# Graph block with batch norm and gated relational layers: loads of x and W on SP's queue and split by partition, turns and x times W earlier, weight merges and parts in other places

## The chip, the cores and the metric

The kernel runs on one core of a Trainium2 chip. The metric is the device time of one execution in microseconds (us). Time of the kernel before: 353.66 us, the median of three runs (353.53 to 355.02). TensorE (PE) multiplies, VectorE (DVE), ScalarE (ACT) and GpSimd (POOL) compute elementwise, SyncE (SP) only issues loads and stores; ScalarE and GpSimd issue some too.

## The reference

625 nodes with 512 features, 20,625 directed edges (`src`, `dst` sorted by `dst`, a type of 0 or 1 each). Cut to what matters:

```python
# layer 0, edges src -> dst
xw  = x @ W.T
deg = segment_sum(1, dst');  dinv = rsqrt(deg)         # dst' also holds one more loop per node
h   = segment_sum(dinv[row] * dinv[col] * xw[row], col) + b
h   = gelu(batch_norm(h, gamma, beta), exact);  x1 = layernorm(x + (h + x))
# layer 1, twice (first with relu behind it)
w[r] = sum_b att[r, b] * basis[b]                      # 2 relations, 30 bases of 512 x 512
msg  = (sigmoid(x_j @ gate_w[r]) * x_j) @ w[r]         # r = type of the edge, x_j = features of dst
out  = segment_sum(msg, src) + x @ root + bias
return layernorm(x1 + out)
```

## The kernel before

Matrix products in 32 bits are made of three: each operand is split into a part `hi` of reduced precision and the rest `lo` (`mm3`, lines 469 to 471).

**The edge stage.** The 20,625 edges are 162 tiles of 128, in 27 groups of 6. For each tile VectorE makes a one-hot matrix of keys (`oh_key`, 128 x 320, line 1037), where a key joins the chunk of the source node (5 chunks of 125 nodes), the type and the place of the destination in a window of 32 nodes that begins at the group's smallest destination (its base). The one-hot of the source's place inside its chunk (`oh_src`) comes from ScalarE for four tiles of a group (`places`, line 773) and from VectorE for two (line 1035). TensorE multiplies the two (line 560) into one of two banks, and VectorE adds the window into the count matrix `B` (`add_window`, line 1022). `oh_key` has 12 slots, `oh_src` three groups. Before the first tile VectorE needs: the edges, turned by TensorE (line 506), the places inside the chunk (line 956 on; ScalarE waits for these), the minimum and maximum of each group (line 967), S, the coefficients for the basis sums (line 975), a few scalars that say whether further rounds are needed (lines 981 to 987), the base on all partitions (lines 524 and 989) and the keys (lines 992 to 998).

**The basis sums** run through the whole kernel. The 64 parts of 1 MB each are loaded by SP's queue into a ring of four (line 371), each load when the part four before it has been used. A part is eight products (`basis_part`, line 476) that TensorE does at written-out places (`basis_upto(n)`). Four parts make a half, eight make one weight block: ScalarE takes the first half out of the bank (`w_first`), VectorE merges the second (`w_merge`, lines 1001 to 1010), ScalarE makes the `hi` part (`w_high`) and VectorE the `lo` part (`w_low`). The first part of a half waits for the half two before it to have left its bank.

**x and W** (the name `W0` in the code, `w_raw` in the profile) are loaded on ScalarE's queue behind the edges (lines 739 and 740), each in one transfer of 125 or 128 partitions. TensorE turns the 5 chunks of x and 4 blocks of W (`turn`) in nine places of the edge loop (`TURN_AT`: after groups 2, 4, 6, ..., 19), ScalarE evicts each one group later (`turned_parts`: a `hi` and a full copy) and GpSimd makes the `lo` part (line 418). x times W is twenty parts, two in each of the groups 14 to 23 (`FIRST_XW`). The first x turn stands after group 2, ahead of its basis part.

**Degrees and z.** From B the adjacency `AT` is made (line 1083), its column sums by TensorE (line 590); VectorE copies them, GpSimd raises five columns to the power -0.5 at once (line 423), VectorE makes the diagonals, ScalarE and VectorE scale x times W (`z`, hi line 827, lo line 1097), TensorE spreads the diagonals (line 600), and the aggregation follows (line 612). Then batch norm, gelu, residual sum, layer norm (five chunks, lines 1154 to 1167), turns of the result x1 (`x1_turned`), its `hi` and `lo` parts, and the products with root (line 652 on), which wait for the `lo` part of the first three chunks.

**The order** is written out by hand on each engine: an engine takes its instructions in order and waits on counters. The psM banks (four) go round in the order of the `use(...)` calls, so a turn also waits until the bank four uses before it has been evicted. The five result chunks are stored from SP's queue, one transfer of 250 KB each, when each is normalised (line 382).

Lines that the steps touch:

```python
340    FIRST_XW = 14
341    TURN_AT = dict(zip((2, 4, 6, 8, 10, 12, 15, 17, 19), range(len(turned))))
408    nc.gpsimd.memset(B[:].bitcast(F32), 0.0).then_inc(consts, 1)
423    nc.gpsimd.tensor_tensor(dinv_p[:], deg[:], mhalf[0:PC, 0:NC], ALU.pow)
567    basis_upto(LEAD + 4 * g // 5)          # LEAD = 3; in the loop over groups g
643    for c in range(EARLY):                 # EARLY = 3
644        x1_turned(c)
645        basis_upto((35, 36, 37)[c])
```

## Time and profile before

| | |
|---|---|
| median of 3 runs | 353.66 us (353.53 to 355.02) |
| the profiled execution | 356.38 us, its span 354.5 us |
| busy, of the span | TensorE 295.9, VectorE 184.2, ScalarE 138.2, GpSimd 51.8 us |
| mean granted clock of TensorE | 0.929 of 2.4 GHz |
| moved by DMA | 73.66 MB, 208 GB/s over the span |

The profile is of one execution; times are from the start of its span. The chain of waits goes back from the last instruction to what released each step; the table by stages gives each engine's busy time in a stretch, the clock that TensorE was granted, the mean share of the core's 16 DMA engines that were busy and the rate. The timeline lists instructions, with like ones merged (x16); in brackets stands how long the engine was idle before and what released it. PE is TensorE's multiplications, PEld its weight loads, ACTq and SPq are the queues of ScalarE and SP.

### The profile page before, as it was taken

The numbers are of one execution on the slowest core, as the hardware profiler recorded it, in microseconds if no ns is written. First come the engines' busy times: TensorE is split into PE (matmuls) and PEld (weight loads), VectorE is DVE, ScalarE is ACT, GpSimd is POOL, SyncE is SP. The second block draws the span as 40 slices with busy tenths as digits, with TensorE's granted clock in tenths as the row PEclk, the third lists the DMA queues.
The fourth block names the chain that finished last, engine by engine and source line by source line (L and its number), as shares of the span: only waits on it lengthen the run. The fifth ranks groups of instructions, "written<-read, shape, count | busy, mean of one in ns | idle before, by whom it ended". The sixth has DMA issues, their size and how long they took to land.

```text
span 354.5 us, 4839 instructions
## 1 busy us (share of the span) xinstructions
PE 295.9 (83%) x1709; PEld 195.7 (55%) x1709; DVE 184.2 (52%) x511; ACT 138.2 (39%) x273; POOL 51.8 (15%) x81
## 2 busy tenths in 40 slices
PE   0662398679999779964899999999999899999980
PEld 0321144346665648742466665556779577777760
DVE  6756079998997864568741013233245325333342
ACT  0064179896997032874823411411131332200000
POOL 5010021311110082027200000000000710010000
PEclk9986579899999759997899999999999999999996
DMA  6799278787577868971999957999200320000111
GB/s 242 292 283 328 96 275 319 251 305 264 203 285 269 325 206 307 336 274 66 329 388 421 379 160 275 358 358 327 92 2 0 87 64 0 2 0 25 32 31 59
DMA packets 12613, 73.66 MB, mean 208 GB/s; under 512 B 1808, under 2 KB 2051, under 8 KB 4396
## 3 DMA queue, kind: packets, MB, share of 16 engines
q1 hardware_dynamic: 9980, 68.49, 53.0%
q0 software_dynamic: 1104, 2.36, 2.5%
q10 hardware_dynamic: 1504, 2.49, 2.2%
q8 instruction: 14, 0.23, 0.3%
q14 instruction: 11, 0.09, 0.1%
HBM read 72.05 MB, written 1.28 MB: 207 GB/s over the span
## 4 chain that ended last, share of the span: by engine, by line
PE 67%; DMA 11%; ACT 7%; DVE 6%; issue 5%; POOL 2%; ACTq 1%; DVEq 0%; POOLq 0%
PE psW L488 15%; DMA xs<-in_x_dram 11%; PE psM L469 10%; PE psM L471 9%; PE psM L470 9%; PE psM L706 6%; PE psM L726 5%; PE psE L560 5%; PE psM L612 3%; ACT oh_diff L776 3%; POOL root_lo L438 1%; DVE AT L1083 1%; PE psM L669 1%; PE psM L639 1%; ACT w L771 1%
## 5 line engine op out<-in xcount | busy, mean ns | idle before, releaser
L488 PE MATMUL psW<-basis_ring,S 128*32 128x512 f32 x512 | 74.1, 671 | 1.6 <-DVEq L980 1.4
L1037 DVE TENSOR_SCALAR oh_key<-iota_f,key 128x320 f16<-128x320 f16 x162 | 45.9, 321 | 20.7 <-PE psE L560 16.9
L1197 DVE SCALAR_TENSOR_TENSOR zg<-psM,gate,zg 125x512 fp32r<-125x512 f32 x20 | 15.0, 750 | 60.3 <-ACT zg L894 60.3
L560 PEld LDWEIGHTS psE<-oh_key,oh_src 128*125 128x125 f16 x162 | 21.7, 148 | 33.9 <-ACT oh_src L782 20.2
L560 PE MATMUL psE<-oh_key,oh_src 128*125 128x320 f16 x162 | 31.5, 333 | 10.5 <-ACT oh_src L782 10.3
L776 ACT ACTIVATE oh_diff<-iota_f,edgeT 128x128 f16<-128x128 f16 x108 | 34.3, 389 | 1.7 <-ACT xT_full L790 0.9
L469 PE MATMUL psM<-w,hlT 128*125 128x512 f32 x80 | 32.7, 409 | 0.1
L894 ACT ACTIVATE zg<-psM,gate 125x512 fp32r<-125x512 f32 x20 | 13.8, 688 | 47.1 <-PE psM L471 46.7
L471 PE MATMUL psM<-w,hlT 128*125 128x512 f32 x80 | 31.6, 395 | 0.0
L470 PE MATMUL psM<-w,hlT 128*125 128x512 f32 x80 | 31.6, 395 | 0.0
L706 PEld LDWEIGHTS psM<-BB,zg 125*128 125x128 f32 x160 | 23.1, 188 | 4.2 <-DVEq L1220 3.4
L488 PEld LDWEIGHTS psW<-basis_ring,S 128*32 128x32 f32 x512 | 12.1, 116 | 23.9 <-issue 21.6
L706 PE MATMUL psM<-BB,zg 125*128 125x320 f32 (+1 forms) x160 | 24.4, 309 | 0.0
L726 PE MATMUL psM<-zg,BB 125*125 125x512 f32 x100 | 24.0, 394 | 0.0
L453 POOL DMA_DIRECT2D root_raw<-in_L_gnn_root_dram x16 | 7.9, 501 | 104.3 <-DVE hlT L1223 104.1
L726 PEld LDWEIGHTS psM<-zg,BB 125*125 125x125 f32 x100 | 18.6, 186 | 4.7
L469 PEld LDWEIGHTS psM<-w,hlT 128*125 128x125 f32 x80 | 14.8, 185 | 11.3 <-issue 5.0
L782 ACT ACTIVATE oh_src<-oh_diff,ones_f 128x512 f16<-128x512 f16 x27 | 19.5, 722 | 0.9
L1020 DVE TENSOR_TENSOR w<-w_both,w 128x512 fp32r<-128x512 f32 x16 | 14.2, 930 | 10.7 <-ACT w L771 10.4
L471 PEld LDWEIGHTS psM<-w,hlT 128*125 128x125 f32 x80 | 14.8, 186 | 3.8
L470 PEld LDWEIGHTS psM<-w,hlT 128*125 128x125 f32 x80 | 14.8, 186 | 3.2
L1035 DVE TENSOR_SCALAR oh_src<-iota_f,edgeT 128x128 f16<-128x128 f16 x54 | 15.3, 283 | 0.5 <-DVE w_both L1008 0.5
(161 smaller groups left out, 445.4 us busy)
## 6 DMA issues: line engine op xcount, KB each, us to landing
basis_ring<-in_L_gnn_basis_dram SPq DMA_DIRECT2D x64, 1024.0 KB, 6.4
root_raw<-in_L_gnn_root_dram POOLq DMA_DIRECT2D x32, 64.0 KB, 2.3
xs<-in_x_dram ACTq DMA_DIRECT2D x1, 1250.0 KB
out_dram<-xs SPq DMA_DIRECT2D x5, 250.0 KB
w_raw<-in_L_gnn_W_dram ACTq DMA_DIRECT2D x1, 1024.0 KB, 39.5
bias_b<-in_L_gnn_bias_dram POOLq DMA_DIRECT2D x1, 250.0 KB, 3.6
rows_i<-in_dst_dram SPq DMA_DIRECT2D x1, 80.0 KB
rows_i<-in_src_dram ACTq DMA_DIRECT2D x1, 80.0 KB
```

The costliest lines, as they stand in the source:

```text
L469: nc.tensor.matmul(o, l_hi, r_hi, start=start, stop=False)
L470: nc.tensor.matmul(o, l_hi, r_lo, start=False, stop=False)
L471: last[0] = nc.tensor.matmul(o, l_lo, r_hi, start=False, stop=stop)
L488: m = nc.tensor.matmul(psW[32 * j:32 * j + 32, cc % 2, :], S[:, cc % 2, cc // CH, q].rearrange("p k r -> p (k r)"), ring[:, n % RING, j, : ...
L560: nc.tensor.matmul(psE[0:PC, g % 2, 0:KEYS], oh_src[:, g % 3, j * P:j * P + PC], oh_key[:, t % OH, :], start=(j == 0), stop=(j == G - 1)). ...
L706: last[0] = nc.tensor.matmul(bank(("h", f, h))[:, 0:n], zg[:, i, d, r, f * P:(f + 1) * P], BB[:, at:at + n], start=(d + r + i == 0), stop= ...
L726: last[0] = nc.tensor.matmul(bank(("out", c))[0:PC, :], BB[:, at:at + PC], zg[:, i, d, r, :], start=False, stop=(d == NC - 1 and r + i == 2))
L776: nc.scalar.activation(oh_diff[:, g % 3, j * P:(j + 1) * P], iota_f[:, 0:P], ACT.Abs, bias=edgeT[:, 0, g * G + j:g * G + j + 1], scale=-1. ...
L782: nc.scalar.activation(oh_src[:, g % 3, 0:GA * P], oh_diff[:, g % 3, :], ACT.Relu, bias=ones_f[:, 0:1], scale=-1.0).then_inc(src_ready, 1)
L1035: v.tensor_scalar(oh_src[:, t // G % 3, t % G * P:(t % G + 1) * P], iota_f[:, 0:P], edgeT[:, 0, t:t + 1], None, ALU.is_equal)
L1037: v.tensor_scalar(oh_key[:, t % OH, :], iota_f[:, 0:KEYS], key[:, t:t + 1], None, ALU.is_equal) \
L1197: link(v.scalar_tensor_tensor(out=zg[:, 1, c, r, :], in0=bank(("Z", L, c, r))[0:PC, :], scalar=gate[:, L, c, r:r + 1], in1=zg[:, 0, c, r, ...
```

## The change

1. The loads of x and W move from ScalarE's queue to SP's, behind the destination edges and ahead of the basis. x is loaded in two transfers (`WIDE` = 112 and 13 partitions), and each of the five stores of the result becomes two in the same way.
2. Turns 0 and 1 (now chunks 0 and 1 of x) stand first on TensorE, ahead of the base product; then the product for the attention coefficients, two turns of W, and the other five turns after groups 0 to 4. ScalarE evicts turns 0 and 1 before the places of group 0, and the others after the places of groups 0 to 6.
3. x times W is in groups 4 to 13. The basis parts run up to `9 * g // 10` after group g, where it was `3 + 4 * g // 5`. Both end at part 23. The first two weight blocks' steps move to later groups, `w_first(2)` behind the loop.
4. ScalarE clears B, before its places; GpSimd did. VectorE waits for it before the first window addition.
5. On VectorE the minima and maxima come ahead of the chunks, and S and the rounds' scalars behind tile 11's keys. S is made by 8 instructions in place of 16 and a clearing.
6. The power for dinv is five instructions, one per column, and the diagonals and z go chunk by chunk behind them. `w_merge(2)` moves from before the copy of the degrees to behind the copies of `dinv_b`.
7. `w_merge(3)` moves from behind chunk 1 of the layer norm to behind chunk 4. On GpSimd the `lo` parts of root: two ahead of the layer norm's chunks, and one each behind chunks 1 and 2 (three ahead and one behind chunk 1 before).
8. Basis parts up to 35 stand ahead of x1's turns; 36 and 37 then fall to the place of 38 and 39.
9. GpSimd's permuted copy of the vectors moves behind its `lo` parts.

```diff
-        turned = [("xT", 0)] + [("w0T", k) for k in range(KC)] + [("xT", c) for c in range(1, NC)]
+        turned = [("xT", 0), ("xT", 1)] + [("w0T", k) for k in range(KC)] + [("xT", c) for c in range(2, NC)]
...
-        FIRST_XW = 14
-        TURN_AT = dict(zip((2, 4, 6, 8, 10, 12, 15, 17, 19), range(len(turned))))
...
-        FIRST_AT = {2: 0, 13: 1, 23: 2}
-        HIGH_AT = {9: 0, 20: 1}
-        MERGE_AT = {8: 0, 18: 1}
-        LOW_AT = {10: 0, 21: 1}
+        FIRST_XW = 4
+        FIRST_TURNS = 4
+        FIRST_AT = {8: 0, 17: 1}
+        HIGH_AT = {13: 0, 22: 1}
+        MERGE_AT = {11: 0, 20: 1}
+        LOW_AT = {14: 0, 23: 1}
...
             edge_rows(sp, 1, dst)
+            for p in (slice(0, WIDE), slice(WIDE, PC)):
+                sp.dma_start(xs[p], x.rearrange("(c p) o -> p c o", p=PC)[p]).then_inc(x_in, 16)
+            sp.dma_start(w0_raw[:], W0.rearrange("(c p) o -> p c o", p=P)).then_inc(w0_in, 16)
...
-                sp.dma_start(out.rearrange("(c p) o -> p c o", p=PC)[:, c], xs[:, c]).then_inc(out_done, 16)
+                for p in (slice(0, WIDE), slice(WIDE, PC)):
+                    sp.dma_start(out.rearrange("(c p) o -> p c o", p=PC)[p, c], xs[p, c]).then_inc(out_done, 16)
...
-            nc.gpsimd.memset(B[:].bitcast(F32), 0.0).then_inc(consts, 1)
...
-            nc.gpsimd.tensor_tensor(dinv_p[:], deg[:], mhalf[0:PC, 0:NC], ALU.pow).then_inc(dinv_ready, 1)
+            for c in range(NC):
+                nc.gpsimd.tensor_tensor(dinv_p[:, c:c + 1], deg[:, c:c + 1], mhalf[0:PC, 0:1], ALU.pow).then_inc(dinv_ready, 1)
...
-            for k in range(KC - 1):
-                root1_low(k)
+            root1_low(0)
+            root1_low(1)
             for c in range(NC):
...
-                if c == 1:
-                    root1_low(KC - 1)
+                if 1 <= c < KC - 1:
+                    root1_low(c + 1)
...
-            basis_upto(LEAD)
+            for i in range(2):
+                turn(i)
+            pe.wait_ge(base_ready, 1)
...
+            for i in range(2, FIRST_TURNS):
+                turn(i)
             for g in range(NG):
...
-                if g in TURN_AT:
-                    turn(TURN_AT[g])
+                if g + FIRST_TURNS < len(turned):
+                    turn(g + FIRST_TURNS)
...
-                basis_upto(LEAD + 4 * g // 5)
+                basis_upto(9 * g // 10)
...
-            pe.wait_ge(diag_ready, 1)
             for h, (c0, c1) in enumerate(((0, 4), (4, NC))):
                 wait_free(pe, ("dinv", h))
                 for c in range(c0, c1):
+                    pe.wait_ge(diag_ready, c + 1)
...
+            basis_upto(35)
             for c in range(EARLY):
                 x1_turned(c)
-                basis_upto((35, 36, 37)[c])
...
-            act.dma_start(xs[:], x.rearrange("(c p) o -> p c o", p=PC)).then_inc(x_in, 16)
-            act.dma_start(w0_raw[:], W0.rearrange("(c p) o -> p c o", p=P)).then_inc(w0_in, 16)
...
+            counts = B[:].rearrange("p s t n -> p (s t n)").bitcast(F32)
+            nc.scalar.activation(counts, ones_f[0:PC, 0:1].broadcast_to(list(counts.shape)), ACT.Copy, scale=0.0) \
+                .then_inc(b_zero, 1)
...
+            turned_parts(0)
+            turned_parts(1)
+            act.wait_ge(place_ready, 1)
             for g in range(NG):
                 places(g)
...
-                if g in EVICT_AT:
-                    turned_parts(EVICT_AT[g])
+                if g + 2 < len(turned):
+                    turned_parts(g + 2)
+            w_first(2)
...
+                if t == 2 * G - 1:
+                    build_S()
+                    rounds()
+                    dve.wait_ge(b_zero, 1)
...
-            w_merge(2)
             wait_full(dve, "deg")
...
             for c in range(NC):
-                last = v.tensor_scalar(diag[:, c, :], ident[0:PC, 0:PC], dinv_p[:, c:c + 1], None, ALU.mult)
-            last.then_inc(diag_ready, 1)
-            for c in range(NC):
+                dve.wait_ge(dinv_ready, c + 1)
+                v.tensor_scalar(diag[:, c, :], ident[0:PC, 0:PC], dinv_p[:, c:c + 1], None, ALU.mult).then_inc(diag_ready, 1)
                 dve.wait_ge(z_hi, c + 1)
...
+            w_merge(2)
...
-                if c == 1:
-                    w_merge(3)
+            w_merge(3)
```

## Rows read from the trace of the kernel before

**Rows 1.** The chain that ended last: start in us, length in us, what.

```profile
3.75 37.80 DMA xs<-in_x_dram
...
114.38 0.97 PE psE L560 x6
...
129.84 1.87 PE psW L488 x8
...
172.28 0.99 PE psW L488 x8
...
174.33 0.39 PE psM L469
```

**Rows 2.** Windows of 1 us: each engine's busy time, clock, DMA share, GB/s.

```profile
36.00:37.00 1.00, 0.00 (x0) 0.00 (x0) 0.00 (x0) 0.00 (x0) 0.00 (x0) 0.50 0.34 139
...
350.00:351.00 1.00, 0.00 (x0) 0.00 (x0) 0.00 (x0) 0.00 (x0) 0.00 (x0) 0.50 0.33 100
```

**Rows 3.** Table by stages: us, busy PE, PEld, DVE, ACT, POOL, clock, DMA, GB/s.

```profile
77.65:110.47 32.82, 32.78 (x197) 20.68 (x198) 29.25 (x103) 28.90 (x69) 3.99 (x3) 1.00 0.70 250
...
157.67:174.33 16.66, 11.05 (x65) 5.15 (x65) 13.95 (x33) 10.31 (x13) 9.60 (x14) 0.80 0.53 191
...
174.33:199.52 25.19, 25.19 (x177) 16.43 (x178) 7.18 (x12) 9.62 (x18) 0.00 (x0) 1.00 1.00 395
```

**Rows 4.** Timeline of the start: start, length, engine, line, what [idle before].

```profile
2.52 2.83 POOL L408 MEMSET B<- 125x3280 f32 x1
...
2.58 2.85 DVE L929 CAST ident<-ident 128x128 bf16<-128x128 f32 x1 [2.44 <-POOL BB L407]
...
4.36 16.35 ACTq L740 DMA_DIRECT2D w_raw<-in_L_gnn_W_dram  x1
...
7.25 0.56 DVE L940 CAST rows_f<-rows_i 81x768 f32<-81x768 int32 x1
...
13.11 1.65 DVE L975 TENSOR_TENSOR S<-mask_k,psM 128x32 f32<-128x32 f32 x16 [0.47 <-PE psM L518]
...
16.13 0.19 DVE L989 COPY base_b<-psM 128x27 f32<-128x27 f32 x1
...
17.98 0.94 DVE L1037 TENSOR_SCALAR oh_key<-iota_f,key 128x320 f16<-128x320 f16 x4
```

**Rows 5.** Timelines of ScalarE and VectorE in the edge stage.

```profile
52.78 1.26 ACT L776 ACTIVATE oh_diff<-iota_f,edgeT 128x128 f16<-128x128 f16 x4
...
55.97 1.28 ACT L776 ACTIVATE oh_diff<-iota_f,edgeT 128x128 f16<-128x128 f16 x4 [0.20 <-ACT w0T_full L790]
...
77.45 0.47 DVE L1027 TENSOR_TENSOR B<-B,psE 125x320 f32 x1
...
79.69 0.48 DVE L1027 TENSOR_TENSOR B<-B,psE 125x320 f32 x1
```

**Rows 6.** Timelines of GpSimd and VectorE in the edge stage.

```profile
75.57 1.27 POOL L418 TENSOR_TENSOR xT_lo<-xT_full,xT_hi 128x500 fp32r<-128x500 f32 x1 [4.99 <-ACTq L795]
...
75.66 1.24 DVE L1035 TENSOR_SCALAR oh_src<-iota_f,edgeT 128x128 f16<-128x128 f16 x1
...
78.51 0.25 DVE L1035 TENSOR_SCALAR oh_src<-iota_f,edgeT 128x128 f16<-128x128 f16 x1
```

**Rows 7.** Timelines of TensorE, VectorE and GpSimd, 120 to 156 us.

```profile
120.24 3.31 PE L590 MATMUL psM<-ones_r,AT 125*125 125x2 f32 x15 [0.19 <-DVE AT L1085]
...
122.19 0.74 DVE L1004 SCALAR_TENSOR_TENSOR w_both<-psW,mask_h,w_half 128x512 f32<-128x512 f32 x1
...
124.60 0.17 DVE L1088 COPY deg<-psM 125x5 f32<-125x5 f32 x1 [0.24 <-DVE w_both L1008]
...
124.99 1.20 POOL L423 TENSOR_TENSOR dinv_p<-deg,mhalf 125x5 f32<-125x5 f32 x1 [24.57 <-DVEq L1090]
...
134.13 0.49 DVE L1119 TENSOR_TENSOR hf<-psM,dinv_b 128x320 f32<-128x320 f32 x1 [2.50 <-PE psM L612]
...
155.48 0.54 POOL L420 TENSOR_TENSOR bn<-bn,mhalf 128x1 f32<-128x1 f32 x1 [2.79 <-DVE bn L1128]
```

More of the change, by code:

```diff
@@ L72 @@
 EPS = 1e-5
+WIDE = PC // 16 * 16
 SWAPPED = [i ^ 1 for i in range(32)]
@@ L242, in gnn_block @@
         use("minmax", "dve")
+        turned = [("xT", 0), ("xT", 1)] + [("w0T", k) for k in range(KC)] + [("xT", c) for c in range(2, NC)]
+        for name in turned[0:2]:
+            use(name, "act")
+        use("base", "dve")
         use("att", "dve")
-        use("base", "dve")
-        turned = [("xT", 0)] + [("w0T", k) for k in range(KC)] + [("xT", c) for c in range(1, NC)]
-        for name in turned[0:KC + 2]:
+        for name in turned[2:]:
             use(name, "act")
@@ L250, in gnn_block @@
             use(("xw", c), "act")
-            if KC + 2 + c < len(turned):
-                use(turned[KC + 2 + c], "act")
         use("vec", "act")
@@ L513, in _ @@
             done()
-            pe.wait_ge(att_in, 16 * 2)
-            pe.wait_ge(spread_ready, SUB)
-            wait_free(pe, "att")
-            for q in range(SUB):
-                last[0] = nc.tensor.matmul(bank("att")[:, 2 * R * q:2 * R * (q + 1)],
-                                           spread[:, q * P:(q + 1) * P],
-                                           att_t[:].rearrange("p l r -> p (l r)"), start=True, stop=True)
-            done()
-            pe.wait_ge(base_ready, 1)
-            wait_free(pe, "base")
-            last[0] = nc.tensor.matmul(bank("base")[:, 0:NG], ones_f[0:1, :], gmm[0:1, 0, :], start=True, stop=True)
-            done()
             def turn(i):
                 what, c = turned[i]
-                pe.wait_ge(x_in if what == "xT" else w0_in, 16)
+                pe.wait_ge(x_in if what == "xT" else w0_in, 32 if what == "xT" else 16)
                 wait_free(pe, (what, c))
@@ L543, in xw_part @@
                 n = slice(c * PC, (c + 1) * PC)
-                pe.wait_ge(in_lo, 2 + k if c == 0 else 1 + KC + c)
+                pe.wait_ge(in_lo, 3 + k if c == 0 else 1 + KC + c)
                 if k == 0:
@@ L550, in xw_part @@
                     done()
-            basis_upto(LEAD)
+            for i in range(2):
+                turn(i)
+            pe.wait_ge(base_ready, 1)
+            wait_free(pe, "base")
+            last[0] = nc.tensor.matmul(bank("base")[:, 0:NG], ones_f[0:1, :], gmm[0:1, 0, :], start=True, stop=True)
+            done()
+            pe.wait_ge(att_in, 16 * 2)
+            pe.wait_ge(spread_ready, SUB)
+            wait_free(pe, "att")
+            for q in range(SUB):
+                last[0] = nc.tensor.matmul(bank("att")[:, 2 * R * q:2 * R * (q + 1)],
+                                           spread[:, q * P:(q + 1) * P],
+                                           att_t[:].rearrange("p l r -> p (l r)"), start=True, stop=True)
+            done()
+            for i in range(2, FIRST_TURNS):
+                turn(i)
             for g in range(NG):
@@ L931, in _ @@
             v.tensor_reduce(mask_h[:], ident[:].rearrange("p (j k h) -> p h j k", j=JB, h=2), AX.XY, ALU.add)
[L932 to L934 removed]
+            v.tensor_reduce(mask_k[:], ident[:].rearrange("p (b k) -> p k b", k=KB), AX.X, ALU.add)
             v.tensor_reduce(pair_sum[:], ident[0:2 * R, 0:2 * R].rearrange("p (i r) -> p r i", r=R), AX.X, ALU.add)
@@ L953, in _ @@
                 dve.sem_inc(free_dve, 1)
+            wait_full(dve, "minmax")
+            for i, op in enumerate((ALU.min, ALU.max)):
+                last = v.tensor_reduce(gmm[0:1, i, :], bank("minmax")[0:1, i * ROWS:(i + 1) * ROWS]
+                                       .rearrange("p (g t) -> p g t", t=G // 2), AX.X, op)
+            link(last)
+            dve.sem_inc(free_dve, 1)
+            dve.sem_inc(base_ready, 1)
             chunk = beyond
```

67 lines of the change are left out of this document (27 added, 40 removed).

## The prediction

> **What bounds the kernel now.** I read the table by stages first, then the chain of waits, then the timeline of each engine where two stages meet. The chain opens with the load of x: issued at 3.75 us, it ends the wait of the tensor engine only at 41.6 [rows 1]. While it finishes alone, the DMA share is 0.34 at 139 GB/s, about 5 of 16 engines; where basis loads fill the queue from 174 us on, the share is 1.00 and the rate 395 GB/s [rows 3]. x's destination has 125 partitions and the outputs' too: near the end the same share, 0.33, at 100 GB/s comes back [rows 2]. W's load, issued behind x on ScalarE's queue, takes 16.35 us to issue and keeps ScalarE from its first instruction [rows 4]. After that come an edge stage of 27 groups of six one-hot products (to 115.4 us [rows 1]), the degree and z stage, the first aggregation, the residual and layer norm, and from 174.33 us a stretch in which the tensor engine is busy all the time [rows 3] to 344.6.
>
> In the edge stage three engines are close. VectorE needs 2.24 us for a group (one window addition to the next, 77.45 to 79.69), ScalarE 3.19 for a group's places with the eviction of one turned chunk (52.78 to 55.97) [rows 5]. The ten groups that also hold x times W took 32.82 us with the tensor engine busy throughout [rows 3]: with them it is the bound.
>
> **1. Loads of x and W** go to SP's queue ahead of the basis and x splits into 112 and 13 partitions. x is 1.28 MB. If the large part uses all engines at 395 GB/s, it takes 3.2 us; issued at about 2.0 to 2.6, and one or two microseconds until data flows and is confirmed (an estimate), it lands near 7.7 (bounds: 6, and 14 if the split does nothing, see the rivals). W needs 1.05 MB more, 2.6 us, and lands near 10.3; basis part 0 near 13. A part of the basis is first wanted at about 18, so the 5 us that it is later costs nothing. SP passes three more issues before its first basis load, ScalarE two fewer. For splitting speaks the low share of both transfers with 125 partitions [rows 2]. The Trainium skill, page "DMA: Bandwidth & Descriptors", section "Why a DMA increments its semaphore by 16 and not by 1", has a load use the largest number up to 16 that divides its outermost size: 5 for 125, 16 for 112, 13 for 13, and the trace agrees with the first. The same page's "Rules for kernel authors" speaks against the change: halves by partition serialize, so one is told not to split; that is a rival below.
>
> **2. Start of VectorE.** Its first cast takes 2.85 us although it is 128 elements wide; it ends with GpSimd's clearing of B, 2.83 us, 2.52 to 5.35 [rows 4]. The clearing moves to ScalarE, idle then; VectorE saves about 2.6. The edge lists are then the limit. They are issued ahead of everything else, and the trace doesn't show when they land, only that the conversion at 7.25 [rows 4] finds them there: it starts between 0 and 2.6 earlier; I take 2.0, near the upper end, as they are small loads, 80 KB each. Building S (1.65) and the rounds' scalars leave the path to the keys: from the start of S at 13.11 to the copy of the base at 16.13, 3.0 us, they are all that stood before the base [rows 4], and S had waited some 0.4 for the attention load. So 3.4 off. First key at 17.98 - 2.0 - 3.4 = 12.6. The base product now stands behind the turns of x chunks 0 and 1, done by about 10 if x lands at 7.7, so it waits for nothing. ScalarE: table load, B, two evictions of turned chunks (until about 12), places of group 0 (about 2): first product at about 14; before, ScalarE's queue was free only at 20.7 [rows 4].
>
> **3. Edge stage.** Groups 0 to 4, by VectorE: two groups without their additions, 2 x (2.24 - 0.47) = 3.5 [rows 5], plus two GpSimd low parts. Such a part slows VectorE: during the one at 75.57 a VectorE instruction that else takes 0.25 takes 1.24 [rows 6], so 1.0 each. 12.6 + 3.5 + 2.0 = 18.1. S and rounds, 3.0: 21.1. Three more groups at 2.24 + 1.0: 30.8. ScalarE needs 3.19 a group and would be at group 4 by 27, the tensor engine likewise: VectorE decides. Group 4's products end at 30.9. The ten groups with x times W (now 4 to 13) hold nine basis parts where they held eight, 32.8 + 1.0, less 1.0 for group 4's own products, already counted: group 14 opens at 63.7. By then VectorE is two groups ahead (twelve key slots). Groups 16 to 26: 11 x 2.24 = 24.6, a weight merge 2.4 [rows 7] and a low part, taken alike, 2.4: 93.1, and 0.5 for the last group. The basis has 12 parts to bring there at 2.6 each, 31 us, mostly ahead in the ring: no bound. **End 93.6 against 115.4: -21.8.** Bounds: 88 (VectorE not slowed by GpSimd, half the S block hidden) and 101 (basis and VectorE waits adding up, 0.5 a group).
>
> **4. z stage.** The merge leaves the path: VectorE copies the degrees at 124.60 after the merge that began at 122.19, but the degree products run until 123.5 [rows 7], so 1.0 comes off, not 2.4. The power of five columns takes 1.21 us [rows 7]; a single one 0.54 [rows 7], so the first result comes 0.7 earlier and the last 1.5 later. VectorE then does diagonal and low z of a chunk in 0.9, so chunk 4's diagonal is ready at 128.7, and after one product and the basis part of 1.87 [rows 1] the aggregation starts at 131.1, where that part ended at 131.7: **-0.6** (bounds -1.5, 0). The merge lands in VectorE's wait of 2.50 us before 134.13 [rows 7]: nothing. Without that wait it would cost 2.4 at the basis part that needs it.
>
> **5. Layer norm.** VectorE has 13.95 us of work in these 16.66 [rows 3], and the low part of turned chunk 2 is what the products at 174.33 [rows 1] wait for. The merge moves from chunk 1 to behind chunk 4, still ahead of that low part: the same work before the same instruction. GpSimd's two low parts later let chunk 0 through 1.3 earlier, but VectorE is still late: 0. Parts 36 and 37 ran here in the tensor engine's idle time and now stand in the stretch where it is always busy: 2 x 0.99 [rows 1] = **+1.9**. And the tensor engine now does its two parts at 160, then only three short turns before 174.3. The mean granted clock of 0.80 over 16.66 us [rows 3] is 6.7 us at 1.2 GHz, at which eight basis products take 1.87 and not 0.99 [rows 1]. Before, basis parts used those slow microseconds up; now root's products meet them, about 5 us at half speed: **+2.5** (bounds 0, 3.3).
>
> **6. End.** Five stores become ten. The last two chunks' 0.5 MB take some 5.1 us at 100 GB/s [rows 2]; over all engines at 395 GB/s 1.3, and one more issue of 0.26: **-3.5** (bounds -2.5, -3.9).
>
> **Sum.** -21.8 - 0.6 + 1.9 + 2.5 - 3.5 = -21.5. The profiled execution took 356.38 us (span 354.5), so 334.9; the median of the runs is 353.66, 2.7 lower, and the same step from there gives **332.2, called 332**.
>
> **Rivals.**
> A. *The edge stage gives back only the wait*: what was late because of x goes, and the earlier start is eaten by VectorE, GpSimd and basis waits. Edge end at 101 or a little later, 14 off the edge stage instead of 22, 339.6. For it: VectorE is busy 29.25 of 32.82 us [rows 3]. Against: twelve slots of slack.
> B. *The split does nothing for the rate*: x alone at 115 GB/s or so takes 11, ahead of the basis in its queue, landing at 13.5; the start shifts by 5.8 and the stores save nothing, 3.5: 332 + 9.3 = 341. By the skill's rule on halves this is the case. Against: share 0.33 [rows 2] leaves eleven engines free.
> C. *Slower than before*: the base product, and so every key, now waits for x, where three groups ran without it. If x still lands at 41.6, sharing engines with W and the basis, the whole edge stage moves by 33.6: 365. It decides once x lands after about 29.5. Against: x is first in its queue, not beside others.
> D. *More than I think*: VectorE runs groups 0 to 4 unslowed and the clock after layer norm costs nothing: 27 off for the edge and 0 for the clock: 324.
>
> **Chances.** Forecast (326 to 336) 0.55, A 0.22, B 0.06, C 0.03, D 0.14. About 0.5% is what a measurement can tell here. Only C is slower; within 0.5% would need A to lose 13 us more, 0.01. So faster 0.96, same 0.01, slower 0.03. Range: from D's edge to A and B, 324 to 342; outside is some 0.12.
>
> **What would show it.** x's turn before 10 us; first one-hot product near 14; ScalarE's queue without a 16 us issue; x times W in groups from 30 to 64; end of the edge stage at 93; VectorE without the 2.85 us cast; in the layer norm a tensor engine idle for some 5 us before root's first products, and those at 1.2 GHz; DMA share in the stores near 1 and the last one done within 2.5 us of the issue. The prediction is wrong if x lands after 12, or if the ten groups with x times W take more than 36, or the last thirteen more than 32.

## The result, and the profile after

The changed kernel took 339.75 us (median of four executions, 338.11 to 342.25), the kernel before 354.34 on the same chip (353.53 to 355.26): a ratio of 0.959, 95% interval 0.953 to 0.966. The forecast was 332 within 324 to 342. The sum was made for one profiled execution each: 356.38 before, 338.11 after, so 18.3 less where 21.5 were forecast. The medians lie only 14.6 apart: the profiled execution before was the slowest of its kernel, the one after the fastest. So the time lies in the stated range, but outside the forecast's own 326 to 336 and next to rival A's 339.6, whose mechanism did not happen (below).

Page of the changed kernel: span, busy time, DMA share in 40 slices.

```profile
span 336.3 us, 4839 instructions
...
PE 295.1 (88%) x1709; PEld 195.7 (58%) x1709; DVE 180.5 (54%) x502; ACT 141.1 (42%) x274; POOL 50.4 (15%) x84
...
DMA  6968799699997898660899678988000410000111
```

TensorE has the same work (295.9 us before), in a span 18 us shorter. Its chain of waits (start, us, what):

```profile
2.39 8.23 DMA xs<-in_x_dram
...
149.91 5.22 issue
...
160.11 5.77 DMA basis_ring<-in_L_gnn_basis_dram
```

The wait for x is 8.2 us long and ends at 10.6; it was 37.8 us long and ended at 41.6 [rows 1]. New are 5.22 us in which TensorE stands still ahead of root's products, and a basis part that it waits for at 166. The timeline of all engines, where stages meet:

```profile
5.10 2.94 ACT L803 ACTIVATE B<-ones_f 125x3280 f32<-125x3280 f32 x1
6.34 0.56 DVE L948 CAST rows_f<-rows_i 81x768 f32<-81x768 int32 x1 [2.35 <-DMA rows_i<-in_edge_type_dram]
...
10.66 1.93 PE L524 MATMUL psM<-ident,xs 125*128 125x125 f32 x8 [2.24 <-DMA xs<-in_x_dram]
13.25 0.19 DVE L981 COPY base_b<-psM 128x27 f32<-128x27 f32 x1 [1.34 <-PE psM L547]
13.58 0.98 DVE L984 TENSOR_TENSOR key<-edgeT,base_b 128x162 f32<-128x162 f32 x1
14.31 1.28 ACT L780 ACTIVATE oh_diff<-iota_f,edgeT 128x128 f16<-128x128 f16 x4 [0.19 <-ACT xT_full L794]
14.60 1.18 DVE L988 TENSOR_SCALAR key<-key 128x162 f32<-128x162 f32 x1
16.54 0.94 DVE L1050 TENSOR_SCALAR oh_key<-iota_f,key 128x320 f16<-128x320 f16 x4
...
22.36 1.94 PE L491 MATMUL psW<-basis_ring,S 128*32 128x512 f32 x8 [2.28 <-DVEq L1001]
...
96.31 0.49 DVE L1040 TENSOR_TENSOR B<-B,psE 125x320 f32 x1 [0.86 <-PE psE L566]
104.41 0.17 DVE L1104 COPY deg<-psM 125x5 f32<-125x5 f32 x1 [1.31 <-PE psM L596]
104.82 3.43 POOL L426 TENSOR_TENSOR dinv_p<-deg,mhalf 125x1 f32<-125x1 f32 x5 [65.47 <-DVEq L1106]
...
166.02 1.07 PE L491 MATMUL psW<-basis_ring,S 128*32 128x512 f32 x8 [0.99 <-DMA basis_ring<-in_L_gnn_basis_dram]
```

And its table by stretches (busy time and instructions of PE, PEld, DVE, ACT, POOL, then granted clock, DMA share, GB/s); the last row is the stores:

```profile
5.00:6.00 1.00, 0.00 (x0) 0.00 (x0) 0.00 (x0) 0.99 (x2) 0.00 (x0) 1.00 1.02 309
...
8.00:9.00 1.00, 0.42 (x4) 0.07 (x1) 0.68 (x3) 0.03 (x1) 0.00 (x0) 1.00 1.19 226
9.00:10.00 1.00, 0.00 (x0) 0.00 (x0) 0.63 (x3) 0.00 (x0) 0.00 (x0) 1.00 1.11 125
...
34.00:44.00 10.00, 10.00 (x61) 5.72 (x60) 9.55 (x30) 9.68 (x25) 3.43 (x3) 1.00 0.78 279
...
64.00:74.00 10.00, 10.00 (x72) 4.46 (x70) 9.23 (x40) 9.32 (x24) 0.00 (x0) 1.00 0.94 338
...
139.23:155.13 15.90, 6.17 (x44) 3.57 (x43) 13.92 (x34) 11.47 (x16) 9.61 (x14) 0.78 0.51 198
155.13:158.63 3.50, 3.50 (x14) 3.46 (x15) 1.99 (x2) 0.13 (x1) 0.00 (x0) 0.53 0.00 0
...
333.00:334.00 1.00, 0.00 (x0) 0.00 (x0) 0.16 (x1) 0.00 (x0) 0.00 (x0) 0.50 0.84 254
```

Between the two profiled executions the difference splits as follows (the first row is a time from the start, the others are lengths; "root to gates" goes from the start of the products with root to that of the gate rows).

| stage | before | after | change | forecast |
|---|---|---|---|---|
| last window addition | 115.48 | 96.31 | -19.2 | -21.8 |
| from there to the copy of the degrees | 9.12 | 8.10 | -1.0 | -1.0 |
| copy of the degrees to the aggregation | 7.04 | 8.04 | +1.0 | +0.4 |
| aggregation to root | 42.69 | 42.68 | 0.0 | 0 |
| root to gates | 25.13 | 29.39 | +4.3 | +4.4 |
| gates to the last normalised chunk | 148.03 | 148.10 | +0.1 | 0 |
| from there to the end of the span | 7.0 | 3.7 | -3.3 | -3.5 |

### The profile page after: what moved, and what is told of

Read it like the earlier page. It is cut to its first block, busy times and chain, and to the rows that moved or that the text cites. A ratio compares the mean times of both kernels' runs of the same rounds, so it can differ in the third digit from the quotient of the medians.

```text
span 336.3 us, 4839 instructions
## 1 busy us (share of the span) xinstructions
PE 295.1 (88%) x1709; PEld 195.7 (58%) x1709; DVE 180.5 (54%) x502; ACT 141.1 (42%) x274; POOL 50.4 (15%) x84
## 3 DMA queue, kind: packets, MB, share of 16 engines
HBM read 72.05 MB, written 1.28 MB: 218 GB/s over the span
## 4 chain that ended last, share of the span: by engine, by line
PE 71%; DVE 13%; issue 6%; DMA 4%; ACT 2%; POOL 2%; DVEq 1%; SPq 0%; POOLq 0%; ACTq 0%
PE psW L491 15%; PE psM L472 10%; PE psM L473 9%; PE psM L474 9%; PE psE L566 7%; PE psM L712 6%; PE psM L732 6%; PE psM L618 3%; DVE oh_key L1050 3%; DMA xs<-in_x_dram 2%; DMA basis_ring<-in_L_gnn_basis_dram 2%; DVE w L1033 1%; PE psM L675 1%; PE psM L596 1%; DVE x_sum L1165 1%
## 5 line engine op out<-in xcount | busy, mean ns | idle before, releaser
L491 PE MATMUL psW<-basis_ring,S 128*32 128x512 f32 x512 | 68.7, 624 | 4.1 <-DVEq L1001 2.3
L1050 DVE TENSOR_SCALAR oh_key<-iota_f,key 128x320 f16<-128x320 f16 x162 | 47.3, 333 | 4.0 <-DVE B L1040 0.8
L566 PEld LDWEIGHTS psE<-oh_key,oh_src 128*125 128x125 f16 x162 | 20.5, 140 | 31.1 <-issue 15.8
L566 PE MATMUL psE<-oh_key,oh_src 128*125 128x320 f16 x162 | 33.0, 323 | 4.6 <-DVE oh_key L1050 3.7
L491 PEld LDWEIGHTS psW<-basis_ring,S 128*32 128x32 f32 x512 | 11.3, 109 | 22.6 <-issue 17.5
L1033 DVE TENSOR_TENSOR w<-w_both,w 128x512 fp32r<-128x512 f32 x16 | 13.2, 862 | 11.5 <-ACT w L775 11.0
L472 PE MATMUL psM<-hlT,root_hi 128*128 128x320 f32 (+1 forms) x32 | 11.3, 353 | 5.2 <-issue 5.2
```

The lines of the kernel that those rows point to most:

```text
L472: nc.tensor.matmul(o, l_hi, r_hi, start=start, stop=False)
L491: m = nc.tensor.matmul(psW[32 * j:32 * j + 32, cc % 2, :], S[:, cc % 2, cc // CH, q].rearrange("p k r -> p (k r)"), ring[:, n % RING, j, : ...
L566: nc.tensor.matmul(psE[0:PC, g % 2, 0:KEYS], oh_src[:, g % 3, j * P:j * P + PC], oh_key[:, t % OH, :], start=(j == 0), stop=(j == G - 1)). ...
L1033: v.tensor_tensor(lo, full, hi, ALU.subtract).then_inc(w_lo, 1)
L1050: v.tensor_scalar(oh_key[:, t % OH, :], iota_f[:, 0:KEYS], key[:, t:t + 1], None, ALU.is_equal) \
```

## The experiments

Each time has the kernel before beside it on the same chip: 355.03 us with runs 1 to 4, 354.41 with 5 to 8, 354.87 with 9 to 11, 354.38 with 12. Ratios are to that; all edits start from the changed kernel unless said.

**1. The changed kernel again.**

> The changed kernel once more, to see how much of the gap between its profiled execution (18.3 us under the profiled one before) and its median (14.6 us under) is the executions and not the change. Theory: the stages of the first profile repeat within 0.5 us up to the end of the edge stage (96.3), the wait for a basis part behind root's second block (1.0 us) is what varies; median 338 to 341. Rival: the edge stage itself varies by 2 to 4 us, with the time at which x lands (10.6).

339.13 us (338.02 to 341.11), ratio 0.955 (0.952 to 0.958). With the first four, its executions spread over 4.2 us, those of the kernel before over 1.7. The trace was of the slowest: edge stage to 98.59, 2.3 later than in the first. The first basis part waits for S, with group 1's products behind it, and starts at 23.86 instead of 22.36; group 5's products start 2.2 later (38.43 instead of 36.19), and that stays. So the rival is right that the edge stage varies, and wrong in its reason: x was turned at 10.74, as before. What landed late are the edge lists:

```profile
8.15 0.56 DVE L948 CAST rows_f<-rows_i 81x768 f32<-81x768 int32 x1 [4.16 <-DMA rows_i<-in_edge_type_dram]
```

In the first trace VectorE had them at 6.34. In this one it reaches the copy of the base at 14.68 without a wait, so here the lists and not x set the first key (16.98). How far each of the lists and the subtractions of GpSimd makes up the 2.3 us no run isolates. The 1.0 us wait for a basis part is absent, yet root to gates still took 29.1 us: the half clock lasted longer (see the layer norm below).

**2. Only the loads and the split**, put into the kernel before:

```diff
+                for p in (slice(0, WIDE), slice(WIDE, PC)):
+                    sp.dma_start(xs[p], x.rearrange("(c p) o -> p c o", p=PC)[p]).then_inc(x_in, 16)
+            sp.dma_start(w0_raw[:], W0.rearrange("(c p) o -> p c o", p=P)).then_inc(w0_in, 16)
-            act.dma_start(xs[:], x.rearrange("(c p) o -> p c o", p=PC)).then_inc(x_in, 16)
-            act.dma_start(w0_raw[:], W0.rearrange("(c p) o -> p c o", p=P)).then_inc(w0_in, 16)
```

and the stores split in the same way.

> The kernel before with the loads of x and W on SP's queue, x and the stores split, and nothing else. Theory (loads carry the change): the tensor engine no longer waits 12.5 us for x in group 2, some 2 us of half clock behind it go too, and the first group is no earlier, since four basis parts now land later: edge stage ends near 101 where it was 115.5 and the changed kernel has 96.3; stores 3.2 off; layer norm as before. Sum 17 off the profiled 356.4: 339 to 340, within 1 us of the whole change. Rival (the new order carries it): with the old order the places, the keys and four basis parts ahead of group 0 keep the start at 28 or later, and the time is 344 or more.

340.87 us (339.62 to 342.14), ratio 0.962 (0.959 to 0.965). The edge stage ended at 102.7, 12.7 earlier than before, with no other edit. The theory had the end near 101 and held within 2 us, the rival (344 or more) falls. So step 1 carries 14.2 of the 15.9 us by which run 1 is ahead of the kernel before; all that steps 2 to 9 add in the edge stage (another 4 to 6 us) is mostly given back in the z stage and at root. Step 1 is three edits at once (SP's queue, ahead of the basis, the split); no run takes them apart in the old order.

**3. Steps 7 and 8 undone** (the merge behind chunk 1 again, GpSimd's low parts, the parts between x1's turns):

```diff
-            basis_upto(35)
             for c in range(EARLY):
                 x1_turned(c)
+                basis_upto((35, 36, 37)[c])
```

> The changed kernel with the layer norm's part undone: the fourth weight merge behind chunk 1, three low parts of root ahead of the chunks, basis parts 35, 36 and 37 between x1's turns. Theory: from the end of gelu to the gates the kernel before took 4.3 us less; undone, it comes back, in three pieces: two parts (1.9), root's first block at 2.4 GHz and not 1.2 (1.5), no wait for a basis part (1.0). Time 4.3 less than the changed kernel. Rival: the loss hangs on the DMA stream being late from the faster edge stage, then only 2 us or less come back. VectorE's end of layer norm doesn't move in either (under 0.5 us).

336.00 us (334.28 to 339.27), ratio 0.950 (0.944 to 0.956): 3.1 us under run 1 where 4.3 were expected, with ranges that overlap. The traces are clearer. Timeline, then table, of this run at root's first products:

```profile
153.22 1.07 PE L491 MATMUL psW<-basis_ring,S 128*32 128x512 f32 x8
155.45 0.39 PE L472 MATMUL psM<-hlT,root_hi 128*128 128x320 f32 x1 [1.17 <-issue]
```

```profile
155.45:158.95 3.50, 3.50 (x28) 2.61 (x32) 2.36 (x3) 3.19 (x6) 0.00 (x0) 1.00 0.96 379
```

TensorE comes from its last basis part with 1.17 us of idle time instead of 5.22, root's products run at 2.4 GHz, and the DMA queue, which stood at share 0.00 in the changed kernel, moves 379 GB/s. The products start at the same time (155.45 and 155.13) and reach the gates in 25.1 us instead of 29.4. The whole +4.3 is these two steps; they were not undone apart from each other, and run 8 shows the gain again beside the power's.

**4. Step 6's power undone**: one instruction on five columns, and the waits that go with it.

```diff
-            for c in range(NC):
-                nc.gpsimd.tensor_tensor(dinv_p[:, c:c + 1], deg[:, c:c + 1], mhalf[0:PC, 0:1], ALU.pow).then_inc(dinv_ready, 1)
+            nc.gpsimd.tensor_tensor(dinv_p[:], deg[:], mhalf[0:PC, 0:NC], ALU.pow).then_inc(dinv_ready, 1)
```

> The changed kernel with one power of five columns, all diagonals first and then z, as before; the third weight merge stays behind. Theory: from the copy of the degrees to the first aggregation took 7.1 us before and 8.1 changed, so undoing it gives 1.0 us. Rival: the merge behind dinv_b's copies delays the aggregation's readers, and the stage stays at 8.1.

337.75 us (337.74 to 338.67), ratio 0.952 (0.950 to 0.954). From the copy of the degrees to the aggregation 6.99 us instead of 8.04; GpSimd's row:

```profile
105.39 1.20 POOL L425 TENSOR_TENSOR dinv_p<-deg,mhalf 125x5 f32<-125x5 f32 x1 [65.15 <-DVEq L1105]
```

1.20 against 3.43 us for five: chunk by chunk loses 1.05 us, what the merge behind it had won.

**5. x and the stores in one transfer each** (`WIDE` gone, the loads still ahead of the basis on SyncE).

```diff
-            for p in (slice(0, WIDE), slice(WIDE, PC)):
-                sp.dma_start(xs[p], x.rearrange("(c p) o -> p c o", p=PC)[p]).then_inc(x_in, 16)
+            sp.dma_start(xs[:], x.rearrange("(c p) o -> p c o", p=PC)).then_inc(x_in, 16)
```

> The changed kernel with x loaded, and each result chunk stored, in one transfer of 125 partitions, everything else as changed. Theory: a transfer of 125 partitions uses 5 of 16 engines; x lands at about 15 to 18 in place of 10.6, the keys, which now wait for it, and with them the whole edge stage move by 5 to 7, and the stores give 3.2 back: 8 to 10 us slower than the changed kernel, 347 to 349. Rival, by the rule in the Trainium skill, page DMA: Bandwidth & Descriptors, section Rules for kernel authors, that partition halves are not worth splitting: within 1 us of the changed kernel.

351.72 us (351.57 to 351.87), ratio 0.993 (0.990 to 0.995): nearly all the gain of the change is gone, more of it than was expected. Chain, then table:

```profile
2.00 19.02 DMA xs<-in_x_dram
```

```profile
5.00:7.00 2.00, 0.00 (x0) 0.00 (x0) 0.00 (x0) 1.99 (x2) 0.00 (x0) 1.00 0.34 123
...
9.00:20.00 11.00, 1.22 (x8) 0.86 (x8) 3.75 (x13) 0.00 (x0) 0.00 (x0) 1.00 1.06 236
...
22.00:24.00 2.00, 2.00 (x10) 1.68 (x9) 0.19 (x2) 1.60 (x4) 0.45 (x1) 1.00 1.07 435
```

x alone gets 0.34 of the engines at 123 GB/s, at which 1.28 MB would take 10.4 us. From about 9 us W and the basis fill all sixteen, but together with x they move only 236 GB/s, where 435 go once x is through, and x lands only at 21.0 instead of 10.6. Why x and the transfers behind it slow each other is not shown. The edge stage ends 10.5 later (106.83), and the last store is done 6.1 us after the last normalised chunk instead of 3.7, another 2.4; together 12.9 of 13.5 us of span. In the changed order every key waits for x, which the kernel before does not, so this is the price of the missing split in the new order only. The Trainium skill, page "DMA: Bandwidth & Descriptors", section "Rules for kernel authors", says that transfers of two halves of the partitions serialize, since both use all 16 engines, so that one should not split. With 125 partitions that premise does not hold (share 0.34), and the run decides for the split; the rule of the same page on the divisor of the outermost size (section "Why a DMA increments its semaphore by 16 and not by 1") is the one that the traces bear out.

**6. The base product ahead of the two turns of x.**

```diff
-            for i in range(2):
-                turn(i)
             pe.wait_ge(base_ready, 1)
             wait_free(pe, "base")
             last[0] = nc.tensor.matmul(bank("base")[:, 0:NG], ones_f[0:1, :], gmm[0:1, 0, :], start=True, stop=True)
             done()
+            for i in range(2):
+                turn(i)
```

> The changed kernel with the base product ahead of the first two turns of x. Theory: the base waits for x's landing at 10.66 and two turns, until 12.5, where the minima are there at 9.6; VectorE gets the base at 11.9 in place of 13.25, and the four instructions of the keys run before GpSimd's first low parts (13.1), which stretched two of them by 1.5. First key at 14.0 in place of 16.5, and as VectorE sets the edge stage throughout, its end moves by 1.5 to 2.5. Rival: ScalarE's places (14.3 to 16.3, behind the two evictions) then set the first group, and ScalarE and the tensor engine the stage: under 0.7 us.

339.12 us (337.58 to 340.04), ratio 0.956 (0.952 to 0.959): nothing; the theory falls, the rival (under 0.7 us) holds. VectorE's timeline:

```profile
14.97 1.81 DVE L1050 TENSOR_SCALAR oh_key<-iota_f,key 128x320 f16<-128x320 f16 x4
...
48.05 0.49 DVE L1040 TENSOR_TENSOR B<-B,psE 125x320 f32 x1 [0.56 <-PE psE L566]
...
96.46 0.49 DVE L1040 TENSOR_TENSOR B<-B,psE 125x320 f32 x1 [0.89 <-PE psE L566]
```

The first key comes 1.6 earlier (14.97 against 16.54), the first product only 0.3 (16.66), since ScalarE evicts the two turns first, and ScalarE then works through to 38 without a gap, 3.19 us a group. The rest of the lead is spent by VectorE: its first four keys take 1.81 us beside GpSimd's first low parts, where they took 0.94, and it waits for TensorE 1.4 us in three places instead of 0.9 in two.

**7. B cleared by GpSimd again**, with VectorE still waiting for it only before the first addition (one execution).

```diff
+            nc.gpsimd.memset(B[:].bitcast(F32), 0.0).then_inc(b_zero, 1)
-            nc.scalar.activation(counts, ones_f[0:PC, 0:1].broadcast_to(list(counts.shape)), ACT.Copy, scale=0.0) \
-                .then_inc(b_zero, 1)
```

> The changed kernel with B cleared by GpSimd as before. Theory: VectorE's casts take 2.8 us again, but the edges landed at 6.3 and VectorE had waited 2.35 for them, so the conversion starts 0.3 to 0.9 later and the base, which waits for x, not at all: no difference over 0.5 us up to the first product. Rival, my prediction's term: 2.0 us on the path to the first key.

340.97 us, with the edge stage ending at 97.5, inside what the changed kernel showed. Timeline of VectorE, ScalarE and TensorE:

```profile
2.57 2.85 DVE L937 CAST ident<-ident 128x128 bf16<-128x128 f32 x1 [2.44 <-POOL BB L409]
...
7.01 0.56 DVE L946 CAST rows_f<-rows_i 81x768 f32<-81x768 int32 x1 [0.46 <-DMA rows_i<-in_edge_type_dram]
...
11.96 1.28 ACT L793 ACT_TABLE_LOAD   x1 [11.96 <-PE psM L525]
...
17.86 1.86 PE L567 MATMUL psE<-oh_key,oh_src 128*125 128x320 f16 x6 [1.00 <-DVE oh_key L1048]
```

The cast takes 2.85 us again, but the conversion waits for the edge lists all the same, and the first key comes at 16.06, no later than in the changed kernel: the rival falls. The first product, though, comes at 17.86, 0.9 later than in the first trace, where the theory allows 0.5, and 0.2 later than in run 9, the latest of the traces with the changed start. The edit has a second effect: the clearing was ScalarE's first computing instruction, and with it ScalarE's table load (1.28 us) ran at 3.80, when ScalarE was idle. Without it the load stands at 11.96, behind x's first turn and ahead of the first eviction, and the places of group 0 begin at 15.77 instead of 14.31. So the clearing's place gave VectorE nothing in this execution, but took 1.3 us off ScalarE's path.

**8. Runs 3 and 4 together.**

> The changed kernel with the layer norm's part and the powers' part undone together. Theory: the two are on one path one after the other and add: 4.3 and 1.0 less than the changed kernel, 333.5 to 335. Rival: the basis loads, asked for earlier by 5 us, fall behind in the gates' and Z's stretch: 3 us or less.

333.39 us (332.90 to 334.18), ratio 0.941 (0.938 to 0.943). 5.7 us under run 1; the two stages took 7.04 and 25.1, so 1.0 and 4.3 of it are where runs 3 and 4 put them.

**9. Nothing behind x in the queue until it has landed.**

```diff
+            sp.wait_ge(x_in, 32)
             sp.dma_start(w0_raw[:], W0.rearrange("(c p) o -> p c o", p=P)).then_inc(w0_in, 16)
```

> The changed kernel with one more wait: SyncE issues W, the basis and the vectors only when both parts of x have landed. In the changed kernel x landed at 10.6, three microseconds later than forecast, with the DMA share near 1 but only 226 to 309 GB/s between 5 and 9 us. Theory (the transfers behind x take engine time from it): x lands at about 8.0 and the first turn starts at about 8.2. Rival (pieces of 2 KB move slowly whatever stands behind them, and the edge lists hold the engines first): x still lands between 9.8 and 10.8. W lands at 12 to 14 either way, so it is late for its first turn and the first basis part at 22 may be late too; the whole kernel then takes 0 to 2 us more than the changed one, 339 to 341.

339.27 us (338.81 to 341.37), ratio 0.959 (0.955 to 0.963). Chain, then table:

```profile
2.38 8.13 DMA xs<-in_x_dram
```

```profile
8.00:9.00 1.00, 0.32 (x3) 0.00 (x0) 0.66 (x2) 0.00 (x0) 0.00 (x0) 1.00 0.93 199
9.00:10.00 1.00, 0.00 (x0) 0.00 (x0) 0.71 (x4) 0.00 (x0) 0.00 (x0) 1.00 0.19 17
...
13.00:14.00 1.00, 1.00 (x7) 1.00 (x6) 0.69 (x2) 1.00 (x2) 0.96 (x1) 1.00 1.05 410
```

The theory falls: x lands at 10.5, alone as in company, as the rival said. But the rival's reason falls too. W moves in pieces of 2 KB as well, and in this run, at 13 to 14 us, when all packets are of that size (200 packets, 0.41 MB), the queue moves 410 GB/s at the same share; x reached 199 to 254 from 6 to 9 us. Why x, in 112 and 13 partitions at the start of the kernel, is slow stays open. At 8 to 9 us the engines show as nearly full at 199 GB/s; the data is through soon after 9, and TensorE is released 1.3 us later.

**10. The low parts of x and W by VectorE** (`in_low(i)`: the same subtraction; four behind the rounds' scalars, one behind each of groups 2 to 6).

> The changed kernel with the nine low parts of x and W made by VectorE (behind the rounds' scalars and behind groups 2 to 6) instead of GpSimd. Each such part should take VectorE 0.55 to 0.65, 5.4 in all, and the VectorE instructions that take 1.2 to 1.5 beside GpSimd's work now should take their 0.25 to 0.5 again. Theory (one low part on GpSimd costs VectorE about 1.0, as forecast): the stretching was 9 us, so VectorE is 3 to 4 us less loaded up to 40 us; but the addition at about 48 waits for TensorE anyway, so the edge stage still ends at 96 to 97 and the whole stays within 1 us. Rival 1 (the stretching costs little in all): VectorE is 3 us more loaded, its waits at 48 to 51 vanish, end at 97.5 to 99.5. Rival 2 (VectorE from the start sets the end): end at 93 to 94.5.

338.06 us (336.42 to 341.05), ratio 0.956 (0.951 to 0.962). VectorE's timeline:

```profile
26.28 0.68 DVE L1044 TENSOR_TENSOR w0T_lo<-w0T_full,w0T_hi 128x512 fp32r<-128x512 f32 x1
...
45.65 0.52 DVE L1052 TENSOR_SCALAR oh_key<-iota_f,key 128x320 f16<-128x320 f16 x2 [0.55 <-PE psE L560]
```

The edge stage ended at 95.4, between theory (96 to 97) and rival 2 (93 to 94.5); the time is within 1.1 us of run 1 with overlapping ranges. VectorE does 5.9 us more of its own and still is ahead: between 44 and 54 us it is busy 7.58 us, not 8.40. From 8 us to its last addition it is busy 77.3 us, 78.4 in the changed kernel's first trace, so GpSimd's nine parts cost it some 6.9 us there, 0.8 each (an estimate). Part of what is freed is waited away behind TensorE.

**11. Run 8 with the second low part outside the edge stage.**

```diff
-        LOW_AT = {14: 0, 23: 1}
+        LOW_AT = {14: 0}
+            w_low(1, (0,))
             wait_full(dve, "deg")
             link(v.tensor_copy(deg[:], bank("deg")[0:PC, 0:2 * NC:2]))
             dve.sem_inc(free_dve, 1)
             dve.sem_inc(deg_ready, 1)
+            w_low(1, (1,))
```

> Steps 6 and 7 undone, and the low part of the second weight block (two instructions of VectorE, 1.94 us together, now in group 23) moved out of the edge stage into VectorE's two waits around the copy of the degrees (1.30 and 1.47 us idle in the kernel with both undone). Theory (VectorE sets the last ten groups, from about 76 us): the last window addition comes 1.7 to 2.0 earlier, at 94.7 to 95.0 instead of 96.65, and the time is 331.5 instead of 333.4. Rival (TensorE with the basis loads sets them, DMA share 1.01 from 74 to 84 us): the end moves by less than 0.5 and the time stays at 333 to 334.

331.04 us (330.75 to 331.53), ratio 0.934 (0.932 to 0.937). VectorE's timeline, then the table:

```profile
95.55 0.49 DVE L1039 TENSOR_TENSOR B<-B,psE 125x320 f32 x1 [1.24 <-issue]
...
103.64 0.17 DVE L1104 COPY deg<-psM 125x5 f32<-125x5 f32 x1 [0.39 <-PE psM L595]
104.05 1.02 DVE L1032 TENSOR_TENSOR w<-w_both,w 128x512 fp32r<-128x512 f32 x1 [0.24 <-DVE deg L1104]
```

```profile
84.00:94.00 10.00, 9.85 (x62) 3.97 (x60) 9.40 (x43) 5.34 (x13) 0.00 (x0) 1.00 0.95 380
```

Both halves of the low part hide in the waits (the first stands at 102.25). The addition comes 1.1 earlier of the 1.7 to 2.0 of the theory: VectorE did set this end, and with 1.9 us less work TensorE, busy 9.85 of 10, is level with it. Run 8's trace has a granted clock of 0.83 in this stretch, this one 1.00; that is not the cause, since the changed kernel's first trace had 1.00 there too and ended at 96.31. The time fell by 2.35, twice that: the aggregation began 6.53 after the degrees instead of 7.04, and all the rest to root took 42.0 instead of 43.3 (155.03 and 111.78, 152.19 and 110.17).

**12. Runs 6, 10 and 11 together.**

> The kernel of the eleventh run (steps 6 and 7 undone, second low part behind the edges) with two more edits: the low parts of x and W by VectorE (tenth run: edge stage ended at 95.4 instead of 96.3 to 96.9) and the base product ahead of the turns of x (sixth run: first key 1.6 earlier, nothing at the end). Theory (each edit takes off what it took alone): the last window addition comes at 94.5, 1.0 before the 95.55 of the eleventh run, and the time is 330.0. Rival (TensorE, busy 9.85 of the 10 us from 84 to 94 in the eleventh run, has become the bound and starts no earlier): end at 95.2 to 95.8 and 331.

330.46 us (329.27 to 332.28), ratio 0.931 (0.928 to 0.934). The end moves to 94.15, more than the theory's 94.5; the rival falls. But the time is only 0.6 lower, inside the ranges. First the table, GpSimd's power and the aggregation's first products in run 11, then the same in this one:

```profile
108.00:112.00 4.00, 4.00 (x25) 2.63 (x24) 3.60 (x7) 0.52 (x1) 4.00 (x9) 0.80 1.06 343
```

```profile
104.05 1.20 POOL L425 TENSOR_TENSOR dinv_p<-deg,mhalf 125x5 f32<-125x5 f32 x1 [63.25 <-DVEq L1106]
...
110.17 3.17 PE L617 MATMUL psM<-AT,z 125*128 125x320 f32 x20
```

```profile
108.00:112.00 4.00, 4.00 (x17) 2.12 (x17) 3.56 (x8) 0.00 (x0) 4.00 (x9) 0.50 0.88 236
```

```profile
102.66 2.04 POOL L419 TENSOR_TENSOR dinv_p<-deg,mhalf 125x5 f32<-125x5 f32 x1 [77.23 <-DVEq L1112]
...
110.15 4.08 PE L611 MATMUL psM<-AT,z 125*128 125x320 f32 x20
```

The 1.4 us won in the edge stage are gone where the aggregation starts (110.15 and 110.17), in this trace, its kernel's slowest. 0.8 of them went in the power, which took 2.04 us instead of 1.20 with the same code and the same subtraction of VectorE beside it; TensorE waits for its result. The other 0.5 went in the basis part ahead of the aggregation, which took 1.94 us where it took 1.42: TensorE, after a wait of 1.78 us instead of 0.93, still has a clock of 0.50 there. From the aggregation to root another 1.4 are lost (43.4 against 42.0).

## Why the prediction was right, and where not

**1. Loads.** The mechanism held (x first, over all engines, ahead of the basis; runs 2 and 5), the size was too good: x lands at 10.6, not 7.7. The failed step is "all engines at 395 GB/s", a rate taken from basis loads [rows 3]. While x came in, the queues moved 309 down to 125 GB/s at a share near 1 (5 to 10 us). Run 9 shows that W behind it takes nothing from it and that the size of the pieces is not the reason; the reason is open. Rival B's price was wrong too: without the split x lands at 21.0 and not 13.5, since the step "x alone at 115 GB/s or so takes 11" held only until W and the basis were in flight (run 5).

**2. Start.** "First key 12.6" became 16.54. The edge lists landed at 6.3 with the conversion 0.9 and not 2.0 earlier [rows 4], and over the traces of all runs they landed between 6.2 and 8.15; in run 7 VectorE, held by the clearing, was ready at 6.5 and still waited for the lists until 7.0. The base product "waits for nothing" was wrong: VectorE waited 1.3 us for it behind x's turns, a result of the late x (but not in run 1, where the lists were late). Two key instructions were stretched to 0.98 and 1.18 by GpSimd's first low parts, which stood in the budget of later groups. The first product came at 16.98 instead of 14. And S left the path to the keys but not that of TensorE: the first basis part waited 2.28 us for it, ahead of group 1.

**3. Edge stage.** The late start of 3 us had shrunk to 1.6 when group 4 began (31.5 against the sum's 29.9), and the ten groups with x times W took 33.7 where 33.8 stood, so group 14 opened at 65.2 against 63.7: ScalarE with 3.19 a group, then TensorE, busy 10.00 of 10.00 us in each ten from 34 to 74, set that stretch; run 6 shows that an earlier VectorE buys nothing there. The step "VectorE decides" failed for the first groups. Groups 14 to 26 took 31.1 to the last addition where 29.9 stood: VectorE's stretch, as forecast and as run 11 shows. So 96.3 against 93.6. Rival A, which ended at 101, came no nearer than run 1's 98.6; that the median nearly equals its 339.6 is chance. The cost of 1.0 us for a GpSimd low part was somewhat high: run 10 puts it at 0.8. None of the forecast's signs of being wrong came (x after 12, more than 36 for the ten groups, more than 32 for the last thirteen).

**4. z stage.** -1.0 for the merge was exact. The five single powers took 3.43 us where the forecast had five times 0.54, so 2.2 longer than one of five (1.20 in its row, not 1.21) and not 1.5, and the effect at the aggregation was +1.0 and not +0.4: 0 in place of -0.6.

**5. Layer norm.** All three parts of the sum are in the trace: VectorE's end unchanged (42.68 against 42.69 from aggregation to root), two parts more, and the half clock: root's first twelve products from 155.13 to 158.46, at a granted clock of 0.53, take 3.3 us, against 1.85 at full clock in run 3 (155.45 to 157.30). That is 1.5, not 2.5. The missing 1.0 is a wait that I had not forecast: with no part used for so long the ring was full, the queue stood idle (share 0.00), and the fifth part after it came too late at 166.02. Right sum, one term too large, one missing, in this trace. In those of runs 1 and 4 TensorE does not wait for that part, and root to gates still takes 29.1 and 29.5 us: there the granted clock stays at 0.50 for some 5 us from root's first product, not 3.5, and less the 1.9 of the two parts the half clock alone costs 2.0 and 2.5. Over all traces that keep steps 7 and 8 root to gates is 28.9 to 30.1 us, so clock and wait together cost 1.9 to 3.1.

**6. End.** -3.3 against -3.5; the stores run at share 0.84 with 254 GB/s where it was 0.33 and 100 [rows 2].

The forecast of 332 was low against the median of 339.75 for two reasons: 3.2 us of the sum (2.6 of them in the edge stage), and the anchor. 2.7 were taken off because the execution before was slow, while the profiled one after was the fastest; the median after is 1.6 above it. That the time still fell into the range is owed to the range's width, which had room for rival A, and not to these steps.

## What to carry to other kernels

Read the DMA share of a transfer before its rate: 0.3 with a partition count that 16 does not divide means that a split at a multiple of 16 is worth trying, most of all when other transfers share its queue. Count for a step moved off one engine's path which other engine still waits for it (S here), and do not leave TensorE without work ahead of a long stretch in which it is the bound: filler parts used in its idle time were free here, kept the clock and kept the ring moving (run 3). When an instruction moves off an engine, look what it brought forward there: the clearing on ScalarE hid a table load of 1.28 us (run 7). The best kernels here, 330.5 to 331 us, keep the loads and the new order of the edge stage and undo the steps in the z stage and the layer norm.

## What the runs showed of the hardware

- A transfer of 125 partitions kept about 5 of 16 engines busy (0.34 at 123 GB/s) and took 19 us for 1.28 MB once full-width transfers were queued behind it; in 112 and 13 partitions it took 8.2 (run 5, changed kernel).
- A DMA share of 1.0 does not mean full rate: while x came in, 199 to 309 GB/s moved at a share near 1, in the basis loads 395 [rows 3]. The size of the pieces does not explain it: W, in pieces of 2 KB like x, moved at 410 (run 9).
- A power on one column took some 0.69 us (3.43 for five) and on five columns 1.20, in one trace 2.04 (run 12).
- GpSimd's subtractions of 1.26 us each stretch instructions of VectorE beside them: a key step that takes 0.24 alone took 1.18. The same subtraction took VectorE 0.68.
- The same three small loads of the edge lists landed at 6.2 to 8.15 us in different traces, always issued first.
- ScalarE's table load takes 1.28 us ahead of its first computing instruction, wherever that stands: 3.80 in the changed kernel, 11.96 in run 7, 20.80 in the kernel before.
- Half clock lasts beyond a wait: twenty aggregation products took 3.17 us in one trace and 4.08, at a granted clock of 0.50, in another with the same code. The clock, the landing of the edge lists and the power's length all differ between traces; which of them makes the wide spread of some of these kernels no run isolates.
